# Two SwiGLU feed-forward stages: the next block's row normalization on VectorE moves from behind part 3 to behind part 1

## The reference

```python
x = x + 0.5 * _L0_ffn_ref(_layernorm(x), w_gate, w_up, w_down)     # stage ("ffn", 0)
x = x + _L0_attn_ref(_layernorm(x), ...)                            # gates, delta
x = x + 0.5 * _L0_ffn_ref(_layernorm(x), w_gate, w_up, w_down)     # stage ("ffn", 1)
x = x + 0.5 * _L1_ffn_ref(...)                                      # binary 0
x = x + _L1_attn_ref(...)                                           # space
x = x + 0.5 * _L1_ffn_ref(...)                                      # binary 1

def _L0_ffn_ref(x, w_gate, w_up, w_down):    # 256 -> 768 -> 256, weights times 1/127
    gate = einsum('bsd,hd->bsh', x, wg)
    up = einsum('bsd,hd->bsh', x, wu)
    h = silu(gate) * up
    return einsum('bsh,dh->bsd', h, wd)
```

## Time and profile of the kernel before

| | |
|---|---|
| median of 3 runs | 1502.01 us (1501.01, 1502.01, 1511.87) |
| the profiled execution | 1511.9 us, of it 1510.1 us from the first to the last instruction |
| mean granted TensorE clock | 0.872 of full speed |
| busy: PE, PEld, DVE, ACT, POOL | 78%, 56%, 67%, 36%, 41% of the span |
| first feed-forward stage | TensorE's first transpose at 39.73 us, last down product about 229.9 us |
| second feed-forward stage | TensorE's first transpose at 1054.54 us, last down product about 1241.5 us |

### The profile page before, as it was taken

The page is one execution under the profiler, slowest core; times in us unless marked ns, Lnnn a source line. Parts: engine busy times, 40 slices in busy tenths (PEclk is TensorE's granted clock), DMA queues, the critical chain, the costliest instruction groups (busy, mean ns, idle before and its releaser), DMA issues. The chain is left out here.

```text
span 1510.1 us, 42845 instructions
## 1 busy us (share of the span) xinstructions
PE 1179.1 (78%) x17314; PEld 850.4 (56%) x17314; DVE 1015.7 (67%) x2796; ACT 540.8 (36%) x1367; POOL 612.7 (41%) x1286
## 2 busy tenths in 40 slices
PE   0788887675688888888888888675888879589968
PEld 0667776532455555565565555454676766335546
DVE  5556656327767877788888867763556654589963
ACT  0221212322445555555555545353222216131033
POOL 1223330064345655656666655333332323240035
PEclk9989995576888999989899888888889998799979
DMA  7000001001222222212222222210000002566002
GB/s 191 0 1 1 1 0 47 7 8 29 57 58 59 53 57 55 49 31 54 57 59 59 59 58 52 57 33 2 1 0 1 1 9 62 149 155 176 23 15 98
DMA packets 192741, 71.23 MB, mean 47 GB/s; under 512 B 139296, under 2 KB 187808, under 8 KB 192544
## 3 DMA queue, kind: packets, MB, share of 16 engines
q1 hardware_dynamic: 190944, 65.87, 18.8%
q10 hardware_dynamic: 1600, 2.62, 0.6%
HBM read 43.03 MB, written 21.23 MB: 43 GB/s over the span
## 5 line engine op out<-in xcount | busy, mean ns | idle before, releaser
L470 POOL TENSOR_TENSOR ffn_H<-ffn_hid,ffn_H 128x512 fp32r<-128x512 f32 x96 | 124.8, 1300 | 270.9 <-DVE ffn_H L445 270.9
L1523 DVE TENSOR_TENSOR delta_tmp<-delta_PR 128x30 f32<-128x30 f32 (+14 forms) x480 | 174.8, 364 | 10.3 <-DVE ln_mean_var L295 0.3
L1525 DVE TENSOR_TENSOR delta_PR<-delta_PR,delta_tmp 128x30 f32<-128x30 f32 (+14 forms) x480 | 171.8, 358 | 11.5
L411 ACT ACTIVATE ffn_silu<-psum 128x512 f32<-128x512 f32 x96 | 57.5, 599 | 206.5 <-PE psum L374 206.5
L441 DVE TENSOR_TENSOR ffn_hid<-ffn_silu,psum 128x512 f32<-128x512 f32 x96 | 66.0, 688 | 88.9 <-PE psum L374 86.8
L374 PE MATMUL psum<-ffn_XT,w_gate 128*128 128x512 f32 x384 | 118.5, 434 | 3.9 <-DVE ffn_XT L433 3.9
L1391 ACT ACTIVATE delta_wide<-delta_S 32x128 f32<-32x128 f32 x256 | 78.5, 307 | 104.5 <-DVE delta_S L1545 51.2
L374 PE MATMUL psum<-ffn_XT,w_up 128*128 128x512 f32 x384 | 114.0, 422 | 0.0
L339 PE MATMUL psum<-consts,ffn_xn 128*128 128x128 f32 x128 | 26.2, 371 | 94.7 <-DVE ffn_xn L311 94.7
L387 PE MATMUL psum<-w_down,ffn_H 128*128 128x256 f32 x768 | 95.8, 285 | 5.3 <-POOL ffn_H L470 5.3
L387 PEld LDWEIGHTS psum<-w_down,ffn_H 128*128 128x128 f32 x768 | 95.1, 191 | 7.4 <-POOL ffn_H L470 6.2
(11 more groups left out here) (273 smaller groups left out, 2690.4 us busy)
## 6 DMA issues: line engine op xcount, KB each, us to landing
within_scratch<-delta_PT SPq DMA_DIRECT2D x128, 64.0 KB, 2.0
delta_PR<-within_scratch SPq DMA_DIRECT2D x16, 512.0 KB, 4.4
inverse_scratch<-delta_PR SPq DMA_DIRECT2D x16, 512.0 KB, 5.3
delta_T<-inverse_scratch SPq DMA_DIRECT2D x128, 64.0 KB, 2.4
space_T<-taps_scratch SPq DMA_DIRECT2D x8, 1024.0 KB, 6.2
X<-taps_scratch SPq DMA_DIRECT2D x8, 1024.0 KB, 9.0
X<-in_x SPq DMA_DIRECT2D x32, 128.0 KB, 10.2
late_X<-X SPq DMA_DIRECT2D x64, 64.0 KB, 2.0
```

The source lines that it names most:

```text
L411: a.activation(M.silu[n % 3], B.bank[n % 2][:], ACT.Silu, scale=1.0 / 127.0).then_inc(S.silu, 1)
L470: g.tensor_tensor(lo.bitcast(F32R), M.hid[n % 3], hi, ALU.subtract).then_inc(S.hid_lo, 1)
L1523: i = v.tensor_tensor(t3, column.to_broadcast([P, j, n_after]), row.to_broadcast([P, j, n_after]), ALU.mult)
L1525: i = v.tensor_tensor(after, after, t3, ALU.add)
```

## The change

`prep` is split into `rows` (the four normalizing instructions and their wait and signal, VectorE only) and `turn` (everything else: TensorE's transposes, ScalarE's copies, VectorE's low parts). `turn(b + 1)` stands where `prep(b + 1)` stood, behind part 3. `rows(b + 1)` stands behind part 1, and from block 1 on behind `down(b - 1)`, which is also written behind part 1. The buffer, the waits, the signals and the instructions are the same ones, and as many.

```diff
-def ffn_order(gate_up, prep, down):
-
-    prep(0)
+def ffn_order(gate_up, rows, turn, down):
+
+    rows(0)
+    turn(0)
     for b in range(NBLK):
         for m in range(MH):
             gate_up(b, m)
-            if m == 1 and b > 0:
-                down(b - 1)
+            if m == 1:
+                if b > 0:
+                    down(b - 1)
+                if b + 1 < NBLK:
+                    rows(b + 1)
             if m == 3 and b + 1 < NBLK:
-                prep(b + 1)
+                turn(b + 1)
     down(NBLK - 1)
...
 def ffn_vector(v, own, B, M, S, run):
...
-    def prep(b):
-        n = blocks + b
+    def rows(b):
         if b >= 1:
-            v.wait_ge(S.xt_ps, 2 * n)
+            v.wait_ge(S.xt_ps, 2 * (blocks + b))
         for j in range(BLK):
             i = normalize(v, B, M.xn[:, j * DM:(j + 1) * DM], B.X, B.MV, BLK * b + j)
         i.then_inc(S.xn, 1)
+
+    def turn(b):
+        n = blocks + b
         for k in range(KD):
             v.wait_ge(S.xt_hi, 2 * n + k + 1)
             v.tensor_tensor(M.XT[b % 2][1][k].bitcast(F32R), B.bank[4 + k][:], M.XT[b % 2][0][k], ALU.subtract).then_inc(S.xt_lo, 1)
```

More of the change, by code:

```diff
@@ L348, in ffn_order, with nothing @@
             gate_up(b, m)
-            if m == 1 and b > 0:
-                down(b - 1)
+            if m == 1:
[3 more added lines that the diff above has]
+                    rows(b + 1)
             if m == 3 and b + 1 < NBLK:
-                prep(b + 1)
+                turn(b + 1)
     down(NBLK - 1)
+def nothing(b):
+    pass
 def ffn_tensor(pe, B, M, S, run):
@@ L390, in down @@
             i.then_inc(S.out_mm, 1)
-    ffn_order(gate_up, prep, down)
+    ffn_order(gate_up, nothing, turn, down)
 def ffn_scalar(a, own, B, M, S, run):
@@ L411, in gate_up @@
         a.activation(M.silu[n % 3], B.bank[n % 2][:], ACT.Silu, scale=1.0 / 127.0).then_inc(S.silu, 1)
-    def down(b):
-        pass
-    ffn_order(gate_up, prep, down)
+    ffn_order(gate_up, nothing, turn, nothing)
 def ffn_vector(v, own, B, M, S, run):
@@ L454, in down @@
             tile_stats(v, own, B, B.X, B.MV, t)
-    ffn_order(gate_up, prep, down)
+    ffn_order(gate_up, rows, turn, down)
 def ffn_gpsimd(g, own, B, M, S, run):
@@ L470, in gate_up @@
         g.tensor_tensor(lo.bitcast(F32R), M.hid[n % 3], hi, ALU.subtract).then_inc(S.hid_lo, 1)
-    def down(b):
-        pass
-    ffn_order(gate_up, prep, down)
+    ffn_order(gate_up, nothing, nothing, nothing)
 def binary_sems(S, sem):
```

## The result

| | before | changed |
|---|---|---|
| median | 1506.94 us (4 runs, 1501.01 to 1515.31) | 1428.15 us (4 runs, 1426.37 to 1431.72) |
| ratio | | 0.948, 95% interval 0.942 to 0.954 |
| profiled execution | 1511.9 us | 1431.7 us |
| its span | 1510.1 us | 1429.9 us |
| mean granted clock | 0.872 | 0.893 |

The change is faster by 5.2%, and the median is within 3 us of the forecast of 1431 us.

What follows compares the result with a forecast made beforehand. TensorE was taken to bound the feed-forward stages, standing still once per block: 49.5 us of wait plus 22.1 of clock, 71.6 off the profiled 1511.9, gives 1440.3; with the median 9.9 lower, 1430.4, put at 1431; range 1418 to 1453.

Steps and rivals of the forecast that it cites:

- The first term: TensorE's wait at the turn for the normalized rows would go: 14 waits of 3.54 us, 49.5 us.
- When the rows are ready: Before the turn: rows ready at about 170.5, at worst 171.4, TensorE there at 171.55; block 0 just fits.
- The second term: Feed-forward blocks would no longer lose granted clock behind the stops at the turn: 22.1 us.
- One sign: Granted clock would be 1.00 from the first block's parts to the end of down(7), but for the start.
- The block's length: From turn to turn a block would take TensorE's busy time at full clock, 17.95 us.
- From 1511.9 to the median: Whole kernel: profiled 1511.9 us becomes 1440.3; carried to the median, 9.9 less, 1430.4; perhaps 1440 if that was clock.
- its own rival: The clock stays bad: time 1452, or 1464 with a drop at every turn; chance 0.09.
- What is late next: Behind the moved rows no new wait: up products 2.4 us to spare, next block's first product 2.2.
- Rival 3: Rows hold back part 2's product and part 4's up products; costs above 3.8 us, break-even 7.3 us; chance 0.02.
- Rival 2: Rows come up to 1 us late per turn, 14 us back, time about 1445; chance 0.07.
- Rivals 1 and 4: Wait goes but clock stays bad, 1452 or 1464, chance 0.09; nothing changes, turn waited for something else, chance 0.02.

Runs made afterwards that it cites:

- e2: The changed kernel with the rows one part ahead of the turn (behind part 2) and not two; 1457.71 us, ratio 0.969.
- e4: Two runs: the changed kernel with the four normalizing instructions done one or three times more first, into a spare buffer; 1442.3 us (single profiled execution) and 1492.54 us.
- e1: The kernel before, with 24 throw-away products on TensorE ahead of each of the 14 waits for the normalized rows; 1486.37 us, ratio 0.988.
- e4_rows_x4: The changed kernel with 12 more normalizing instructions ahead of the real four, into spare buffers (blocks 1 to 7), 5.3 us expected; 1492.54 us, ratio 0.991.
- e3: The changed kernel with the rows behind part 1 but ahead of the down products' evictions on VectorE; 1447.93 us, ratio 0.962.
- e6: The changed kernel with throw-away products at each feed-forward stage's start, 18 ahead of the first turn and 8 behind it; 1428.42 us, ratio 0.948.
- r1: The changed kernel as it is, timed again beside e7 on one chip; 1436.49 us, ratio to before 0.954.
- e7: The kernel of e6, with down(7) doing parts 0 to 4 of its first two tiles before waiting for part 5; 1426.88 us, ratio 0.945.
- r2: The kernel of e7 timed again on the same chip as the changed kernel; 1426.29 us, ratio to before 0.946.
- e5: The changed kernel with every transpose of a turn done four times over into the same place; 1475.89 us, ratio 0.981.

## Why the prediction was right, point by point

- *The first term, the wait.* 14 waits of 3.54 us, 49.5 us. Right: none is left, and e2 and e4 show that TensorE waits just as long as the rows are late.
- *When the rows are ready.* 1.38 us at the new place with GpSimd idle, as taken from the earlier trace rows, and ready 0.9 us ahead of the turn, where I said 1.1. In block 0, beside GpSimd, 2.36 us: ready at 53.77, with TensorE there at 53.83. It fitted, as said, with nothing to spare. What no row of before could show was the rounding behind part 3's product: it now meets GpSimd's work of part 2 and took 0.79 us here and up to 1.03 elsewhere (L452: longest 1026 ns, against 594 before). It is hidden.
- *The second term, the clock.* 22.1 us forecast; e1 gave back 21.8 between second turn and down(7), and 17 in the medians. Right in mechanism and size. One sign was wrong: I said that the clock would be 1.00 to the end of down(7). It was up to down(7), and 0.77 in it, in both stages of the changed kernel. I had not counted the stop of 2.64 us ahead of it, which stands in both kernels. Of the gain it takes 1.5 us in one stage, where the kernel before had kept its clock.
- *The block's length.* Forecast 17.95 us (17.9 to 18.1 as the sign to look for), measured 17.72: the mis-sized term. TensorE's busy time of a block with a stop holds the end of the last product ahead of the stop (0.17 us) and a start of the transposes (0.06 us) that otherwise lie beside other work. That is 2.6 of the 3.3 us by which the stages gained more than I said (37.8 + 37.1 against 71.6); the rest lies ahead of the second turn.
- *From 1511.9 to the median.* The forecast left open whether the median run had lost less clock. The medians differ by 78.8 us in the first series and 69.4 in the second, on both sides of 71.6, so the whole gain shows there too. That the time came within 3 us is partly luck: the median of before was 1506.94 in the end and not the 1502.01 I started from, the gain was 7 us larger than forecast, and the two nearly cancel. The profiled execution, for which the working gives 1440.3, took 1431.7; 3.3 of these 8.6 us lie in the stages, the rest in parts that the change doesn't touch. The range was also drawn too narrow for its own rival: with a drop at every turn the working gives 1464, and the range ended at 1453.
- *What is late next.* Nothing, as said. The low parts were ready at 110.1; the next block's first product needed them at 111.73, 1.6 us later, where I said 2.2.
- *Rival 3, slower than before,* did not come, but its working was wrong. I had the price begin when the four instructions take over 3.8 us, at the up products of part 4. But the same delay holds back the turn too, and TensorE comes to the up products that much later. The price begins at the turn, at 2.3 us, and the up products are never late, as e4_rows_x4 shows. By my estimate the point at which the kernel would be slower than before lies near a group of 2.3 + 3.5 = 5.8 us, and not at 7.3; e4_rows_x4, at 5.3 us, is 0.9% faster.
- *Rival 2,* a new wait of some 1 us, did not come in the changed kernel. e3 has one, though not at the turn: there the rows delay the down tiles. *Rivals 1 and 4* fall with e1 and with the waits.

## What to carry to other kernels

When an engine stops once per loop for a short step of another, look at where that other engine stood idle within the same round, and check the step's inputs and buffer there: moving it by program order alone costs nothing and gave 5% here. Count the clock with the stop: the stops of 3.54 us cost almost half as much again in clock, while those of 1.8 us cost only themselves. The place must be chosen against both neighbours, since one part later cost 28 us of the gain and a few instructions earlier cost 15, both by the length of the stages.

## What the runs showed of the hardware

- Stops of TensorE of 0.7 and 1.8 us ahead of the turns never lowered the granted clock (28 of them in e1 and e2). Those of 2.85 us lowered it in 7 of 12 (e4_rows_x4), those of 3.54 us in 10 of 14 (before; the earlier trace rows has one that did not, at 153.61).
- The stop of 2.64 us ahead of down(7) lowered it in 14 of 20 stages (before, changed, e1 to e6 and r1). Down(7), 48 products, took 5.96 or 5.97 us where the clock was 1.00, and 7.22 to 7.52 where it was 0.77 to 0.80. In e7 and r2, where the stop is 0.78 us, the clock stayed at 1.00 in all four stages.
- 32 f32 transposes in a row, 3.65 us, kept the clock at full speed at all 14 turns of e5.
- The granted clock in a view can mislead at the program's start: in the changed kernel the first eight products from 44 us on followed each other at 0.43 to 0.47 us, in a stretch shown with a clock of 1.00. In e7, with work ahead of them, it was 0.23 to 0.26.
- Four normalizing instructions take 1.38 us with GpSimd idle, and 2.3 to 2.36 with one GpSimd work of 128x512 beside them; that work grew from 1.28 to 1.38 us as well.
